# Skipping empty expert tiles at run time in a fused attention and mixture-of-experts layer

## What is computed

```python
# linear attention, 16 heads of 64, causal, in chunks of 128 positions
q, k, v = phi(x @ Wq.T + bq), phi(x @ Wk.T + bk), x @ Wv.T + bv     # phi = elu + 1
num = tril(q @ k.T) @ v + q @ S          # S: running sum of k.T @ v
out = num / sum(q * (cumsum(k) + z))     # z: running sum of k
x = layernorm(x + out @ Wo.T + bo)
# experts: 8, the best two per token, weighted by their softmax gates
gates = softmax(x @ gate_w.T + gate_b)
top_gates, top_idx = top_k(gates, 2)
x = layernorm(x + sum_over_2(top_gates * (x @ expert_w[top_idx].T + expert_b[top_idx])))
```

## Time and profile before

| what | value |
|---|---|
| time, median of 3 runs | 1055.18 us (1052.9 to 1058.24) |
| the profiled execution, its own time | 1053.25 us |
| its span on the slowest core (core 7) | 1051.7 us |
| spans of the eight cores | 1034.6 to 1051.7 us |
| busy: PE, PE weight load | 924.8 us (88%), 469.0 us (45%) |
| busy: DVE, ACT, POOL | 592.6 (56%), 544.8 (52%), 436.4 us (41%) |
| DMA | 203.01 MB, mean 193 GB/s |

### The profile page before, as it was taken

How to read it: one execution, slowest core, us unless ns; L and a number is a source line. 1 busy time by engine, 2 the same in 40 slices (tenths; PEclk the granted TensorE clock), 3 DMA queues, 4 the chain that set the end, 5 groups by cost and what they waited for, 6 DMA issues and landing times.

```text
span 1051.7 us, 21731 instructions; the slowest of 8 cores (1034.6 to 1051.7 us)
## 1 busy us (share of the span) xinstructions
PE 924.8 (88%) x6837; PEld 469.0 (45%) x6837; DVE 592.6 (56%) x1267; ACT 544.8 (52%) x731; POOL 436.4 (41%) x676
## 2 busy tenths in 40 slices
PE   4799899999999999999999972799999797989883
PEld 1245455454555544545554541444444343434331
DVE  4334766766766766767667775110010487677774
ACT  0654656675756657566566643122222565556562
POOL 9100443533533534334313423423332466667564
PEclk9899999999999999999999996799999899899997
DMA  9989698996976987968726999878996478788761
GB/s 140 159 132 298 145 209 148 154 181 141 184 152 146 158 168 138 193 139 137 179 71 187 270 285 299 263 205 211 265 224 182 142 232 286 254 263 258 257 231 38
DMA packets 101211, 203.01 MB, mean 193 GB/s; under 512 B 31502, under 2 KB 45998, under 8 KB 101104
## 3 DMA queue, kind: packets, MB, share of 16 engines
q0 software_dynamic: 53872, 128.90, 56.2%
q1 hardware_dynamic: 47232, 72.73, 24.0%
HBM read 149.31 MB, written 97.01 MB: 234 GB/s over the span
## 4 chain that ended last, share of the span: by engine, by line
PE 53%; DMA 19%; ACT 8%; DVE 8%; issue 7%; POOL 3%; SPq 1%; DVEq 0%; ACTq 0%; POOLq 0%
PE PS L312 21%; PE PS L967 13%; PE PS L550 11%; DMA out<-AR 5%; DMA AR<-xfd 5%; ACT AR L328 3%; DMA W<-xt 2%; ACT AR L329 2%; DMA y2d<-AR 2%; DMA AR<-xs 1%; PE PS L470 1%; DVE W L333 1%; DVE AR L420 1%; PE PS L596 1%; PE PS L464 1%
## 5 line engine op out<-in xcount | busy, mean ns | idle before, releaser
L312 PE MATMUL PS<-W 128*128 128x512 bf16 x1536 | 362.2, 385 | 28.5 <-DVE acc L269 15.0
L967 PE MATMUL PS<-W,AR 128*128 (+1 forms) x1248 | 290.1, 389 | 1.5 <-issue 1.5
L312 PEld LDWEIGHTS PS<-W 128*128 128x128 bf16 x1536 | 143.9, 99 | 196.0 <-issue 48.9
L967 PEld LDWEIGHTS PS<-W,AR 128*128 128x128 bf16 x1248 | 120.6, 100 | 151.7 <-issue 26.0
L333 DVE SCALAR_TENSOR_TENSOR W<-AR 128x512 bf16<-128x512 f32 x128 | 88.5, 692 | 151.1 <-ACT AR L329 151.0
L328 ACT ACTIVATE AR<-PS,cbs 128x512 f32<-128x512 f32 x128 | 87.8, 686 | 92.1 <-PE PS L312 85.0
L550 PE MATMUL PS<-W 128*128 128x512 bf16 x512 | 118.5, 385 | 3.8 <-DVE ixf L640 3.2
L208 POOL DMA_INDIRECT xs<-AR x32 | 34.5, 1078 | 182.0 <-DVE rden L482 143.4
L1058 ACT ACTIVATE AR<-PS 128x1024 f32<-128x1024 f32 x39 | 39.9, 1024 | 129.0 <-PE PS L967 129.0
L1021 DVE COPY AR<-PS 128x1024 bf16<-128x1024 bf16 x24 | 16.6, 692 | 134.8 <-PE PS L1016 134.8
L329 ACT ACTIVATE AR<-PS,cbs 128x512 f32<-128x512 f32 x128 | 87.7, 685 | 0.0
(11 more groups left out here) (127 smaller groups left out, 1318.5 us busy)
## 6 DMA issues: line engine op xcount, KB each, us to landing
AR<-xfd SPq DMA_DIRECT2D x39, 524.0 KB, 5.9
AR<-AR SPq DMA_DIRECT2D x32, 512.0 KB, 5.3
AR<-x POOLq DMA_DIRECT2D x32, 512.0 KB, 7.8
escr<-ew POOLq DMA_DIRECT2D x64, 256.0 KB, 9.4
W<-escr SPq DMA_DIRECT2D x40, 256.0 KB, 8.2
W<-xt POOLq DMA_DIRECT2D x64, 128.0 KB, 6.9
AR<-xs SPq DMA_DIRECT2D x24, 260.0 KB, 4.6
W<-escr SPq DMA_DIRECT2D x48, 128.0 KB, 7.4
```

What stands on the lines that cost most here:

```text
L312: return Q.op("PE", lambda e: e.matmul(bank(b), lt, rh, start=(k == 0), stop=(k == KB - 1)), inc="cpe" if k == KB - 1 else None)
L967: mm = e.matmul(bank(2 * pi + hh), xTb[i][:, k * 128:(k + 1) * 128], w, start=(lst == 1 and k == 0), stop=(k == KB - 1))
```

## The change

1. `count_tiles`: DVE stores the number of tiles of each list (`ntile`, one more instruction), and PE, DVE, ACT and POOL each load both counts into registers before the second list.
2. `Streams.tile(lst, t)`: what PE, DVE and ACT do for tile t of a list, for t of 32 and up (seven tiles in each list), is put under a condition. Each run of instructions with one condition becomes an `If`: with fewer than t+1 tiles the engine only waits for what these instructions would have waited for and raises the semaphores that they would have raised; `Else` holds the instructions. POOL skips only the three small operations of the first list. POOL's scatters and gathers and all of SP's loads are still issued for every tile.
3. First list: the gather is made two tiles ahead, not three.
4. Attention loop, before `late`: `stage_rank` and `stage_scatter` of chunk g-3 both move behind `stage_numden` and the unit after it.
5. Beginning: the load of `cbc` waits until the sixth `Wq` slice has landed; PE's wait for the constants moves behind the opening units; ACT does one Exp at once (which loads its table); `Wk` gets a semaphore for each slice, and units 8 to 15 are done slice by slice like the first eight.

```diff
+    @contextmanager
+    def tile(self, lst, t, engines=("PE", "DVE", "ACT")):
+        if t < S // 128:
+            yield
+            return
+        outer = {k: dict(self.seen[k]) for k in engines}
+        self.cond = {k: (lst, t) for k in engines}
+        yield
+        self.cond = {}
+        self.seen.update(outer)
...
+    def emit(self, eng, e):
+        for cond, group in groupby(self.q[eng], key=lambda x: x[0]):
+            group = list(group)
+            if cond is None:
+                for _, fn, _ in group:
+                    fn(e)
+                continue
+            with e.If_lt(self.count[(eng, cond[0])], cond[1] + 1):
+                for _, _, sem in group:
+                    if sem:
+                        h, val, k = sem
+                        if val > 0:
+                            e.wait_ge(h, val)
+                        if k:
+                            e.sem_inc(h, k)
+            with e.Else():
+                for _, fn, _ in group:
+                    fn(e)
...
     v_cb = dma("SP", "dcb", cb[:], dcb)
-    v_bo = dma("SP", "dbo", cbc, dbo)
...
+    Q.wait("SP", first[5])
+    v_bo = dma("SP", "dbo", cbc, dbo)
...
-    for k in range(KB):
-        wk_tok = dma("POOL", "dk", wcol(1, k, 0, DM), dw[1][:, k, :])
+    wk_tok = [dma("POOL", f"dk{k}", wcol(1, k, 0, DM), dw[1][:, k, :]) for k in range(KB)]
...
+    v_eps = Q.op("DVE", lambda e: e.memset(epst[:], EPS), inc="cdv")
+    Q.wait("ACT", v_eps)
+    Q.op("ACT", lambda e: e.activation(first_exp[:], epst[:], AF.Exp), inc="cac")
...
-    Q.wait("PE", v_const, v_cc)
...
+    def units_by_k(s, u0, toks):
+        done = [None] * 8
         for i in range(8):
-            done[i] = unit_mm(0, i, i, k)
-    for i in range(8):
-        unit_out(0, i, i, done[i])
...
+            Q.wait("PE", *bfree[i])
+        for k in range(KB):
+            Q.wait("PE", toks[k])
+            for i in range(8):
+                done[i] = unit_mm(s, u0 + i, i, k)
+        for i in range(8):
+            unit_out(s, u0 + i, i, done[i])
...
+    units_by_k(0, 0, first)
+    units_by_bank(1, range(0, 8), xt_tok[1])
+    units_by_k(0, 8, wk_tok)
+    units_by_bank(0, range(16, 18), wv_tok)
+    Q.wait("PE", v_const, v_cc)
...
         if not late:
             nxt()
-            if on(3):
-                stage_rank(g - 3)
...
-        if on(3):
-            if late:
-                stage_rank(g - 3)
+        if on(3) and late:
+            stage_rank(g - 3)
             stage_scatter(g - 3)
...
         nxt()
+        if on(3) and not late:
+            stage_rank(g - 3)
+            stage_scatter(g - 3)
         if on(0) and g < NCH - 1:
             stage_state(g)
...
+    for eng in ("PE", "DVE", "ACT", "POOL"):
+        Q.wait(eng, v_tab)
+        for lst in range(2):
+            Q.count_tiles(eng, lst, ntile[0:1, lst:lst + 1])
...
         if t + 1 < NT and turned(t + 1):
-            turn_second(t + 1)
-        vpe = expert_mm(t, 1, pi)
...
+            with Q.tile(1, t + 1):
+                turn_second(t + 1)
+        with Q.tile(1, t):
+            vpe = expert_mm(t, 1, pi)
...
-    for t in range(3):
+    for t in range(2):
         gather_y2(t)
...
-        if t + 3 < NT:
-            gather_y2(t + 3)
+        if t + 2 < NT:
+            gather_y2(t + 2)
         if t + 1 < NT:
-            turn_first(t + 1)
+            with Q.tile(0, t + 1):
+                turn_first(t + 1)
         if t + 2 < NT:
-            cast_first(t + 2)
+            with Q.tile(0, t + 2):
+                cast_first(t + 2)
```

More of the change, by code:

```diff
@@ L1164, in build @@
-        Q.wait("POOL", ve)
-        vr = Q.op("POOL", lambda e, x=x: e.tensor_tensor(
-            rstd[x][:], rstd[x][:], nht[:], ALU.pow), inc="cpl")
-        Q.wait("POOL", vr)
-        vn[t] = Q.op("POOL", lambda e, x=x: e.tensor_scalar(
-            nmr[x][:], mnv[x][:, 0:1], rstd[x][:, 0:1], -1.0, ALU.mult, op1=ALU.mult),
-            inc="cpl")
+        with Q.tile(0, t):
+            pi, i, j, x = t % 3, t % NXF, t % NY, t % 3
+            val = XF[i][:, 0:1024]
+            vpe = expert_mm(t, 0, pi)
+            Q.wait("DVE", g_tok[t], xf_tok[t], xb_tok[t])
+            v1 = Q.op("DVE", lambda e, i=i, j=j, val=val: e.scalar_tensor_tensor(
+                val, Y[j], XF[i][:, F_GATE + 1:F_GATE + 2], val, ALU.mult, ALU.add), inc="cdv")
+            g_free[j] = v1
+            Q.wait("DVE", vpe, v1)
+            v2 = Q.op("DVE", lambda e, i=i, pi=pi, val=val: e.scalar_tensor_tensor(
+                val, PS[:, pi * 1024:(pi + 1) * 1024], XF[i][:, F_GATE:F_GATE + 1], val,
+                ALU.mult, ALU.add), inc="cdv")
+            pair_free[pi] = [v2]
+            Q.wait("DVE", v2, st_free[x])
+            for hh in range(2):
+                vb = Q.op("DVE", lambda e, i=i, x=x, hh=hh: e.bn_stats(
+                    lnst[x][:, hh * 6:(hh + 1) * 6], XF[i][:, hh * 512:(hh + 1) * 512]),
+                    inc="cdv")
+            Q.wait("DVE", vb)
+            va = Q.op("DVE", lambda e, x=x: e.bn_aggr(mnv[x][:], lnst[x][:]), inc="cdv")
@@ new lines, in build @@
+        with Q.tile(0, t, ("POOL",)):
+            Q.wait("POOL", va, st_free[x])
+            ve = Q.op("POOL", lambda e, x=x: e.tensor_tensor(
+                rstd[x][:], mnv[x][:, 1:2], epst[:], ALU.add), inc="cpl")
+            Q.wait("POOL", ve)
+            vr = Q.op("POOL", lambda e, x=x: e.tensor_tensor(
+                rstd[x][:], rstd[x][:], nht[:], ALU.pow), inc="cpl")
+            Q.wait("POOL", vr)
+            vn[t] = Q.op("POOL", lambda e, x=x: e.tensor_scalar(
+                nmr[x][:], mnv[x][:, 0:1], rstd[x][:, 0:1], -1.0, ALU.mult, op1=ALU.mult),
+                inc="cpl")
@@ L1176, in _ @@
         def _(eng):
-            for f in Q.q["PE"]:
-                f(eng)
+            Q.emit("PE", eng)
         @block.vector
         def _(eng):
-            for f in Q.q["DVE"]:
-                f(eng)
+            Q.emit("DVE", eng)
         @block.scalar
         def _(eng):
-            for f in Q.q["ACT"]:
-                f(eng)
+            Q.emit("ACT", eng)
         @block.gpsimd
         def _(eng):
-            for f in Q.q["POOL"]:
-                f(eng)
+            Q.emit("POOL", eng)
         @block.sync
         def _(eng):
-            for f in Q.q["SP"]:
-                f(eng)
+            Q.emit("SP", eng)
     es.close()
```

92 lines of the change are left out of this document (40 added, 52 removed).

## The result

The changed kernel takes **1070.26 us** (median of 4 runs, 1067.95 to 1072.0) beside 1056.71 us for the kernel before in the same comparison: a ratio of **1.0139, 95% interval 1.0095 to 1.0183**. It is slower by 1.4%, where the prediction said 2.8% faster (1026 us, range 1009 to 1043). In some executions the cores of a die ran at a lower clock and longer; all ratios here leave those out, while a median is over all of a kernel's executions. The profiled execution took 1072.0 us, its slowest core 1070.5.

A forecast was written before the change was run, and what follows sets the result against it. PE was taken to bound the attention loop, a ring of scatters, loads and gathers the first list. Core 2: +6 - 10 - 4 - 12.7 - 7.3 + 4 = -24.0, span 1022.6; plus 3.5 gives 1026 us, range 1009 to 1043.

The forecast's parts named there:

- Attention loop: Rank moved behind numden: PE's waits for one-hot and bank go, the mask's wait succeeds them; 10 us gained, bounds 0 and 19.
- The term 19 x 0.53: Attention loop: PE can come 0.53 us earlier in each of 19 chunks before the mask holds it, 10 us.
- Rival B: More comes free: both PE waits in the attention loop won in full, xt arrives earlier; 1013 us, chance 0.10.
- Branches: Conditional groups in both lists, 28 on ACT: 4 us cost taken, lower bound 0, upper 59 us.
- Rival C: Slower: each taken branch fetches instructions, 31 to 59 us instead of 4; 1053 to 1081 us, chance 0.07.
- Who is slowest: Whole kernel: a core with few empty tiles becomes slowest; core 2 at 1022.6 us, core 7 at 1016.
- Beginning: Units 8 to 15 slice by slice: eight outputs end together, k transposes end at about 82.2, not 76.2; price +6 us.
- Second list: Skipping empty tiles brings the end of the second list forward: 9.2 us gained on core 7, some 4 on core 2.
- Steady part: First list, tiles 7 to 34: gather two ahead, 5.15 us a tile instead of 5.62, 12.7 us gained.
- Rival A: The first list keeps its pace, as the gather with less lead stalls DVE; 1039 us, chance 0.14.
- rival D: The skip does nothing, because empty tiles' loads, gathers and scatters are still issued and end the lists; 1037 us, chance 0.07.
- Tail: End of first list: last scatter starts 14.8 us behind tile 34's L1150 on core 7; gain 13.7 us, 7.3 on core 2.

The follow-up runs named there:

- f1: Changed kernel with rank and scatter directly behind numden, ahead of the unit, and ACT's work out of the conditions: 1039.96 us, ratio 0.9868.
- e1: Kernel before with only the attention loop edit (rank and scatter moved behind numden and the unit after it): 1074.41 us, ratio 1.0229.
- e3: Changed kernel with rank and scatter directly behind numden, but ahead of the unit: 1047.65 us, ratio 0.9965.
- f6: f2 with counts stored 32 too high, so conditions on PE, DVE and POOL never skip: 1042.59 us, ratio 0.9906.
- f3: f2 without any condition, all 39 tiles of both lists computed, no branch: 1039.18 us, ratio 0.9871.
- f5: f2 with ACT back under the conditions and counts stored 32 too high, so nothing is skipped: 1057.2 us, ratio 1.0058.
- f2: f1 with units 8 to 15 done bank by bank again: 1030.38 us, ratio 0.9789.
- f4: f2 with the gather three tiles ahead again: 1043.26 us, ratio 0.9899.
- e4: Changed kernel with ACT's work out of the conditions (ACT computes empty tiles too): 1060.78 us, ratio 1.0105.

## Why the prediction was wrong

The forecast was 44 us too low. Its sum was made for core 2, a span of 1022.6 us. That came out at 1050.6, 28.0 more, and the loop, +21.7 instead of -10, is 31.7 of it; the other terms together did 3.7 better than forecast. The time is set by core 6, 19.9 us behind core 2, though it was 9.7 ahead of it before. Its excess comes from several places: it gained 7 us less in the second list (though three tiles are empty there and on core 2 two) and 5.5 less in the steady part, and the tiles from 31 to the end, of which one is empty and on core 2 three, got 9.5 us longer where core 2's got 6.3 shorter. The table loads stand there: tile 31 to the end takes 61.0 us on core 6 in the changed kernel and 49.4 in f1, where ACT is free of conditions (and PE's granted clock is 1.00 in tiles 31 to 37, not 0.88). One profile of each kernel doesn't part these shares more finely.

**Attention loop: the step that failed.** "The banks handed out shift by one, so both waits go." Both did go, and the successor that the prediction named, the mask, came. But the sentence stops where it should have begun to count. A ring of four that shifts by one gives every taker behind the rank another bank, and the one with the least slack (the output projection, 0.4 us behind the end of a unit) got the bank with the longest emptying, two ACT passes of 0.69. This could have been read beforehand: the 1.3 us for the two passes stands in the prediction's own part on the beginning, and the order of the takers is in the code. 24 waits of 1.1 us are the 27.4 us. e1 shows that the edit alone does it, e3 that the bank order does. Freed of it, the move brought 4 us against 10. The term 19 x 0.53 was too large by itself as well. In the kernel before PE began the second half of the numerator 0.53 us behind the mask, as the prediction read, and so it did in every chunk but each fourth (1.7 to 2.1 there). In e3 it begins each half 0.15 us behind its half of the mask and no sooner, so 0.38 was there to win and not 0.53. And it waits at both halves, 0.2 and 0.5 us, where the prediction counted the second alone with 0.4. The forecast left PE 19.2 - 10 = 9 us of waits; in e3 they are 12.3 + 1.8 + 0.7 = 14.8: the mask's in 34 places (17 iterations), the bank that the rank itself frees late (L727), and one for L479. Rival B, both waits won in full, falls with this.

**Branches: the second step that failed.** "I take 4 us", 28 groups at hundredths of a us. The conditions of PE, DVE and POOL are near that (3.7 us, f6 over f3, unresolved). ACT's are not: each group that is carried out begins with a table load of 1.28 us, and in the first list ACT has three groups a tile. That is some 10 us with the empty tiles as they are (f1 against e3) and 15 to 16 where nothing is empty (f5 against f6), and not the 27 x 1.28 = 34.6 us that ACT spends on loads behind branches, since some of them fall where ACT would have waited. Rival C had the place and, by luck, nearly the price of one group (1.1 to 2.1 us), but its mechanism was instruction fetches, and these are few: the page's two queues of instruction fetches show 62 and 51 packets after, 61 and 46 before. Its sum, 31 to 59 us, was not reached. That short forward jumps are cheap held (0.02 us between ACT's groups in the rows above). Nothing in the prediction asked what the compiler adds at a branch.

**Who is slowest.** "A core with few empty tiles slowest" was right, and worse than put: a core with few empty tiles pays for its conditional tiles and gets little back. Core 6, 15 us ahead of the slowest in the profile before (1036.9 us), got the loads and a single empty tile.

**Beginning: right in kind and size.** +6 was forecast; chunk 4 starts 3.6 (core 7) and 6.1 us later (core 6), 5.4 on average over the cores. The last transpose of k was put at 82.2 and came at 80.98 (core 7). Part of that is not what the sum had: PE's first matmul on the second block of xt, forecast at the same time, started at 41.07 us and not 39.87. f2 against f1 gives 8 to 10 us for doing units 8 to 15 slice by slice, of which 5.6 are seen at chunk 4.

**Second list: right in kind.** -9.2 forecast on core 7, -11.8 measured; core 2, with two empty tiles, -10.0 against -4; core 6, with three, -3.0. So close a hit on core 7 is in part luck: over the kernels that skip, this stretch took 135.7 to 146.2 us on core 7, over those that don't 147.3 to 150.1. In f1 and f2, with ACT copying every tile, the average over the cores is 146 us against 150.8 before.

**Steady part: right.** 5.15 us a tile forecast, 5.17 measured on core 7; -12.6 over tiles 7 to 31, where the forecast comes to -11.3. Averaged over the cores a tile took 5.56 us before and 5.14 after. f4 shows that the gather's lead does it. Rival A (the pace is kept) and rival D (the skip does nothing) fall with f4 and with f3 against f2.

**Tail: right in kind, 2.7 us short.** The last scatter stands 1037.79 - 1020.3 = 17.5 us behind the last real tile's addition on core 7, forecast 14.8. POOL's timeline (start, duration, what, idle before) has the difference:

```profile
1030.61 0.99 POOL L258 DMA_INDIRECT out<-AR  x1 [0.27 <-issue]
1034.61 0.98 POOL L258 DMA_INDIRECT out<-AR  x1 [3.01 <-DVEq L124]
1036.55 0.97 POOL L258 DMA_INDIRECT out<-AR  x1 [0.96 <-ACTq L124]
1037.79 0.97 POOL L258 DMA_INDIRECT out<-AR  x1 [0.27 <-DMA out<-AR]
```

The scatters were to follow one another as issues of 1.33 us. Instead two of them wait, 4.0 us together, for a semaphore that another engine raises for a skipped tile (L124 is the line that raises it, in the `If`). A skipped tile still waits for all that its instructions would have waited for. f2 has 17.4 us there too, so it isn't the table loads; which of a skipped tile's waits comes last I did not settle.

**The sum that would have been right.** With both faults mended, f1 took 1040 us against 1026 forecast, 1.3% under the kernel before and not 2.8%: the loop gives 4 us and not 10, the tail 3 less; the rest of the difference is spread over terms of a few us that one profile each doesn't separate.

## What to carry to other kernels

- Where buffers or banks are handed out in turn, an edit that moves or adds one taker changes the buffer of every taker behind it. Write the ring out before and after, and put beside each taker how long ago its new buffer was filled and how long its reader needs. Moving two matmuls of 128x16 cost 22 us.
- Leave an engine that runs activations out of a data-dependent skip unless it has at least the table load (1.28 us here) to spare at each group; let it work on stale data. (One group a tile instead of three should cost less; it was not tried.) Look in the profile for instructions that nobody wrote, and count them.
- The gain of a skip is set by the core that skips least, and its cost is highest there.
- An engine that runs out of work can lose its clock as well: PE's was 0.88 in the tiles that waited for ACT and 1.00 in the same tiles before.

## What was not expected of the hardware and the compiler

- A table load of 1.28 us stands at the head of every stretch of ACT work that begins at or behind a branch, 27 on core 6 in the changed kernel, though one load had served all the functions before. With ACT out of the conditions (e4, f2) there is one.
- Conditional groups on PE, DVE and POOL cost almost nothing: with some 50 of them carried out and nothing skipped, 3.7 us in all, within the spread.
- One bank of 128x512 read twice by ACT (0.69 + 0.68 us, 1.3 together) is enough to stall PE 1.1 us, 24 times in the loop, if the next large step falls on that bank.
